# Feed-forward gates one place sooner and the Gelus moved ahead of the output copies of unit 1, in a two-network attention kernel

## The chip, the cores and the metric

The kernel runs on one core of a Trainium2 chip. The metric is device time in microseconds (us) of one execution. The runs shown are three, and their median is the time before.

## What is computed

The input x is 16 sequences of 128 tokens with 128 channels. Four blocks follow one another: a small cross-attention, a network of six layers, a second cross-attention, and a network of two layers. The change is in the feed-forward of the first network, whose layer is this (shortened):

```
for i in range(6):
    x = attn_layer(shift_tokens(x), Wqkv[i], q_scale[i], k_scale[i], Wo[i]) + x
    x = ffn_layer(shift_tokens(x), ln_g[i], ln_b[i], W1[i], b1[i], W2[i], b2[i]) + x

def attn_layer(x, ...):            # 16 heads of 64, windows of 32 tokens
    q, k, v = split(x @ Wqkv)      # l2norm, scale, rotary on q and k
    return local_attention(q, k, v) @ Wo

def ffn_layer(x, ...):             # DIM_INNER = 341
    xn = layernorm(x) * g + bln
    a, gate = split(xn @ W1 + b1)
    return a * gelu(gate) @ W2 + b2
```

All of it is float32.

## The kernel before

Every engine runs a program written out by hand, and the engines meet by semaphores alone. The first network runs as 96 pairs (6 layers of 16 sequences) in a software pipeline of steps. Step s starts pair s and works at the same time on pairs s-1, s-2 and s-3. A pair has two units, 0 and 1, of eight heads each. All five engines have a function `step_0(s)` that lists their work of a step in order.

TensorE (`step_0`, from L962) issues in step s: keys and queries of unit 0 for pair s (L710), values of unit 0 for s-2, the transposes of the probabilities of unit 1 for s-3 (L776), slot 0 of the feed-forward, the turn of q of unit 0 for s-1 (`turn`, L731), scores (L761, L767) and values (L790) of unit 1, keys and queries of unit 1 (L710), the output projection of s-3 (`project_out`, L823), slot 1 of the feed-forward, the turn of k of unit 0 (L731), probabilities of unit 0 (L776), values of unit 1 (L710), slot 2 of the feed-forward, the turns of k and q of unit 1 (L731, eight transposes), and scores and values of unit 0 (L767, L790).

ScalarE (`step_0`, from L1633) issues in step s: the exponents of unit 0 (`exponents_all`, L1578, eight activations, each with a read of its accumulator), a copy of the values (L1598), a copy of the turned probabilities (L1586), two squares (L1549), the copy of the turned q of unit 0 (`turned`, L1555), the output copies of unit 1 (`outputs(1, s-3)`, L1609, two halves), an activation for the feed-forward where the step has one (L1617, L1624), the exponents of unit 1, two squares, the copy of the turned k of unit 0, the copies L1586 and L1598, the two turned copies of unit 1, and last the output copies of unit 0.

Three of its waits matter here. TensorE begins `project_out` of s-3 only when `outputs(1, s-3)` is done (AT["oe"][1]). It begins the turn of k of unit 1 only when the turned k of unit 0 has left bank 6 (AT["kte"][0]). It begins the values of unit 0 of the next step only when `outputs(0, s-2)` is done (AT["oe"][0]), and the scores of unit 1 of the next step when the exponents of unit 0 have been read from banks 3 and 4.

The feed-forward of four sequences (a group, f = 0 to 23) takes four steps, by the counter c = (s-7) % 4, and shares PSUM bank 2 with a Newton iteration of VectorE:

- c = 0: mean (L835), down-projection of the group before (L877), variance (L841).
- c = 1: slot 0 the broadcast of the inverse deviation (L849); slot 2 gate 0 (`ff_gate`, L859, one product of 128x512 as two matmul records), which VectorE copies to SBUF (L2252).
- c = 2: slot 0 gate 1, slot 1 gate 2. At the end of the step, after the turned copies and before `outputs(0, s-2)`, ScalarE applies the three Gelus (`ff_gelu`, L1631). A Gelu needs another activation table than the exponents: a load ahead of the Gelus and one ahead of the next exponents.
- c = 3: the three up-projections (L868), one a slot, which VectorE multiplies by the Gelus (L2258).

22 groups (f = 0 to 21) run through all four steps while every pair is live; group 22 runs in the last steps, and group 23 in a list by hand (`between`) beside the second cross-attention. `normal_free` makes a product in bank 2 wait for the Newton iteration of the step before, and `ff_done` makes the Newton iteration wait until VectorE has copied the product before it.

```python
if c == 2 and f >= 0:
    ff_gelu(f)            # ScalarE, L1672: behind turned(1, s-1, 0)
if live(s - 2):
    outputs(0, s - 2)
```

Of the kernel before, what the change touches and what calls it, by code (L numbers as in the profile page):

```python
# [63 lines left out]
def build(nc, A, out):  # L64
# [9 lines left out]
    with ExitStack() as ctx:  # L74
# [234 lines left out]
        def g_broadcast(pe, n, k, o):  # L309

            pe.wait_ge(ln_rsqrt, (n + 3) * RSQ)
            pe_broadcast(k, o)
# [263 lines left out]
        def _(pe):  # L576
# [125 lines left out]
            def pe_phase(ph):  # L702
# [191 lines left out]
                def feed_forward_0(s, slot_):  # L894

                    if 1 <= s < 7:
                        group_norm(s, slot_)
                    c, f, before = ff_phase(ph, s)
                    if c == 0 and f >= 0 and slot_ == 0:
                        ff_mean(f, s)  # L900
                    if c == 0 and before >= 0 and slot_ == 1:
                        ff_down(before, s)
                    if c == 0 and f >= 0 and slot_ == 2:
                        ff_var(f)
                    if c == 1 and f >= 0 and slot_ == 0:
                        ff_broadcast(f, s)
                    if c == 1 and f >= 0 and slot_ == 2:
                        ff_gate(f, 0, s)
                    if c == 2 and f >= 0 and slot_ < 2:
                        ff_gate(f, 1 + slot_, s)  # L910
                    if c == 3 and f >= 0:
                        ff_up(f, slot_, s)

# [410 lines left out]
            def between(s, part):  # L1324

                if (s, part) == (1, 1):
                    ff0(99, 0)
                    ff0(99, 1)
                if (s, part) == (1, 2):
                    ff0(99, 2)  # L1330
                if (s, part) == (2, 1):
                    ff0(100, 0)
                    pe.wait_ge(FF["outer"], 3)
                    g_mean(pe, 6, 2, 6)
                if (s, part) == (2, 2):
                    g_var(pe, 6, 2, 6)
                    ff0(100, 2)
                if (s, part) == (3, 0):
                    g_broadcast(pe, 6, 2, 6)
                    ff0(101, 0)  # L1340
                if (s, part) == (3, 1):
                    ff0(101, 1)
                if s == 4:
                    ff0(102, part)
                if (s, part) == (5, 0):
                    ff0(103, 1)
                if (s, part) == (5, 1):
                    pe.wait_ge(FF["outer"], 4)
                    g_mean(pe, 7, 3, 2)
                if (s, part) == (5, 2):  # L1350
                    g_var(pe, 7, 3, 2)
                if (s, part) == (6, 1):
                    g_broadcast(pe, 7, 3, 2)
                if s in (7, 9):
                    n = 8 + (s - 7) // 2
                    if part == 0:
                        pe.wait_ge(LN["xn"], NBLK + n)
                        pe.wait_ge(YP["gt"], 8 * (n - 7))
                        g_mean(pe, n, n - 8, 2)
                    if part == 1:  # L1360
                        g_var(pe, n, n - 8, 2)
                    if part == 2:
                        g_broadcast(pe, n, n - 8, 2)
# [87 lines left out]
        def _(act):  # L1451
# [89 lines left out]
            def act_phase(ph):  # L1541
# [92 lines left out]
                def step_0(s):  # L1634
                    c, f, before = ff_phase(ph, s)
                    if live(s - 2):
                        exponents_all(0, s - 2)
                        values(0, s - 2)
                    if live(s - 3):
                        probs_all(1, s - 3)  # L1640
                    if live(s):
                        square(0, s, 1)
                        square(0, s, 0)
                    if s == 0:
                        gate_weights()
                    if live(s - 1):
                        turned(0, s - 1, 0)
                    if live(s - 3):
                        outputs(1, s - 3)
                    if s in (1, 3, 5):  # L1650
                        g_square(act, (s + 1) // 2, (s + 1) // 2)
                    if c == 0 and f >= 0:
                        ff_square(f)
                    if c == 1 and f >= 0:
                        ff_affine(f)
                    if live(s - 2):
                        exponents_all(1, s - 2)
                    if live(s):
                        square(1, s, 1)
                        square(1, s, 0)  # L1660
                    if live(s - 1):
                        turned(0, s - 1, 1)
                    if s == hi:
                        for k in range(2):
                            g_square(act, 4 + k, k)
                    if live(s - 2):
                        probs_all(0, s - 2)
                        values(1, s - 2)
                    if live(s - 1):
                        turned(1, s - 1, 1)  # L1670
                        turned(1, s - 1, 0)
                    if c == 2 and f >= 0:  # L1672
                        ff_gelu(f)
                    if live(s - 2):
                        outputs(0, s - 2)

# [357 lines left out]
        def _(dve):  # L2034
# [76 lines left out]
            def dve_phase(ph):  # L2111
# [27 lines left out]
                def ff_done(s):  # L2139

                    c, f, before = ff_phase(ph, s)
                    if f < 0 or c < 0:
                        at(dve, FF["z"], before + 1)
                    elif ni == 0 and c == 0:
                        dve.wait_ge(FF["rstd"], RSQ * (f + 1))
                    elif c == (3 if ni == 0 else 1):
                        dve.wait_ge(FF["hid"], 3 * f + 3)
                    else:
                        dve.wait_ge(FF["ge"], 3 * f + (3 if c == 2 else 1))

                n_s, n_b, n_c = (bank[2][:, 64 + 32 * k:96 + 32 * k].rearrange("p (i n) -> p i n", i=2) for k in range(3))

# [124 lines left out]
                def feed_forward_0(s, slot_):  # L2277

                    if 1 <= s < 7:
                        group_norm(s, slot_)  # L2280
                    c, f, before = ff_phase(ph, s)
                    if c == 0 and f >= 0 and slot_ == 0:
                        ff_centre(f)
                    if c == 0 and before >= 0 and slot_ == 1:
                        ff_close(before)
                    if c == 0 and f >= 0 and slot_ == 2:
                        ff_newton(f)
                    if c == 1 and f >= 0 and slot_ == 0:
                        ff_normalise(f)
                    if c == 1 and f >= 0 and slot_ == 2:  # L2290
                        ff_gate(f, 0)
                    if c == 2 and f >= 0 and slot_ < 2:
                        ff_gate(f, 1 + slot_)
                    if c == 3 and f >= 0:
                        ff_hidden(f, slot_)

# [300 lines left out]
            def between(s, part):  # L2597

                if (s, part) == (1, 1):
                    ff0(99, 0)  # L2600
                    ff0(99, 1)
                    outer(PHASES[0], 2)
                if (s, part) == (1, 2):
                    ff0(99, 2)
                if (s, part) == (2, 1):
                    ff0(100, 0)
                    g_centre(dve, 6, 2, 6)
                if (s, part) == (2, 2):
                    g_newton(dve, 6, 2, 6)
                    ff0(100, 2)  # L2610
                if (s, part) == (3, 0):
                    g_normalise(dve, 6, 2, 6)
                    ff0(101, 0)
                if (s, part) == (3, 1):
                    ff0(101, 1)
                if s == 4:
                    ff0(102, part)
                if (s, part) == (5, 0):
                    ff0(103, 1)
                    outer(PHASES[0], 3)  # L2620
                if (s, part) == (5, 1):
                    g_centre(dve, 7, 3, 2)
                if (s, part) == (5, 2):
                    g_newton(dve, 7, 3, 2)
                if (s, part) == (6, 1):
                    g_normalise(dve, 7, 3, 2)
                if s in (7, 9):
                    n = 8 + (s - 7) // 2
                    if part == 0:
                        g_centre(dve, n, n - 8, 2)  # L2630
                    if part == 1:
                        g_newton(dve, n, n - 8, 2)
                    if part == 2:
                        g_normalise(dve, n, n - 8, 2)
# [63 lines left out]
```

## Time and profile before

| | |
|---|---|
| time before, median of 3 runs | 2301.66 us (2299.51 to 2307.42) |
| the profiled execution | 2299.02 us |
| its span | 2297.2 us |
| TensorE busy | 2124.9 us, 93% |
| VectorE busy | 1760.9 us, 77% |
| ScalarE busy | 1712.2 us, 75% |
| GpSimd busy | 1340.2 us, 58% |
| granted TensorE clock, mean | 0.987 |

The span is the time from the first to the last instruction of the profiled execution; the 1.8 us between it and the execution's own time lie outside the instructions. Busy time of an engine is the sum over its instructions. Matmuls overlap the one before a little, so two rows of the timeline can start before the row above has ended. An idle time stands in brackets with what ended it.

### The profile page before, as it was taken

Reading aid. Unit: us, or ns where it says so; the run is one execution under the profiler, and the core shown is the slowest. Engines: PE = TensorE matmul, PEld = TensorE weight load, DVE = VectorE, ACT = ScalarE, POOL = GpSimd, SP = SyncE. Lnnn points to the kernel's source line nnn. Section 1 sums busy time; section 2 is a strip of 40 time slices with the busy share of each in tenths; the row PEclk is TensorE's granted clock in tenths of the full one; section 3 lists DMA queues with packets and bytes.
Section 4 is the critical chain, followed back from the end, with each engine's and each line's share of the span. In section 5 each row is a group of like instructions: output and inputs, shape, how many; then the busy total and the mean of one; then the engine's idle time right before and its main releaser. Section 6 shows DMA issues by size and latency. Waiting matters only on the chain. (4 is left out here: it accounts for less than half of the span.)

```text
span 2297.2 us, 88445 instructions
## 1 busy us (share of the span) xinstructions
PE 2124.9 (93%) x33790; PEld 1456.7 (63%) x33790; DVE 1760.9 (77%) x4953; ACT 1712.2 (75%) x5916; POOL 1340.2 (58%) x1270
## 2 busy tenths in 40 slices
PE   7988999999999999999999999999999886899997
PEld 5656666666666666666666666666666564666665
DVE  4988877778777878777778777877777478788873
ACT  3767788787787877787887777887788543778784
POOL 1337666666666666665676566666666124766660
PEclk8999999999999999999999999999999998999999
DMA  4001221112211222112211122111221100000001
GB/s 112 4 3 39 70 58 45 41 46 67 57 43 39 64 51 57 39 43 61 57 46 42 43 65 60 46 39 45 52 53 43 48 10 10 13 13 16 13 9 28
DMA packets 144799, 96.93 MB, mean 42 GB/s; under 512 B 61976, under 2 KB 137408, under 8 KB 144384
## 3 DMA queue, kind: packets, MB, share of 16 engines
q1 hardware_dynamic: 143232, 91.02, 15.5%
q8 instruction: 274, 4.49, 0.8%
q14 instruction: 141, 1.16, 0.2%
q10 hardware_dynamic: 1152, 0.26, 0.1%
HBM read 23.11 MB, written 1.05 MB: 11 GB/s over the span
## 5 line engine op out<-in xcount | busy, mean ns | idle before, releaser
L710 PE MATMUL bank<-wqkv,hs 128*128 128x512 f32 x1344 | 666.7, 614 | 19.3 <-ACT arena L1609 13.7
L1931 POOL TENSOR_TENSOR arena<-arena,rnorm 128x512 f32<-128x512 f32 x448 | 455.5, 1046 | 388.5 <-DVE rnorm L2180 387.3
L1924 POOL TENSOR_TENSOR arena<-arena 128x512 f32<-128x512 f32 x448 | 568.0, 1275 | 132.5 <-DVE arena L2129 132.2
L1578 ACT ACTIVATE arena<-bank,amx 128x64 f32<-128x64 f32 x1536 | 458.8, 336 | 8.5 <-DVE amx L2195 8.3
L2124 DVE TENSOR_TENSOR arena<-bank,rot 128x512 f32<-128x512 f32 x448 | 306.9, 685 | 82.7 <-PE bank L710 79.0
L1555 ACT ACTIVATE arena<-bank 128x512 f32<-128x512 f32 x448 | 264.4, 617 | 132.0 <-PE bank L731 130.9
L710 PEld LDWEIGHTS bank<-wqkv,hs 128*128 128x128 f32 x1344 | 228.6, 191 | 203.8 <-issue 154.9
L1578 ACT ACTIVATION_READ_ACCUMULATOR arena<-bank,amx 128x1 f32 x1536 | 352.3, 229 | 0.0
L2129 DVE TENSOR_TENSOR arena<-bank,rot 128x256 f32<-128x256 f32 x896 | 334.0, 414 | 0.0
L731 PEld LDWEIGHTS bank<-ident,arena 128*128 128x128 f32 x1792 | 212.6, 142 | 152.8 <-issue 128.3
L2136 DVE TENSOR_REDUCE ss<-arena 128x8 f32<-128x512 f32 x448 | 283.4, 670 | 32.5 <-ACT arena L1549 32.3
L1549 ACT ACTIVATE arena<-bank 128x512 f32<-128x512 f32 x448 | 265.9, 647 | 42.0 <-DVE arena L2129 41.2
L1938 POOL TENSOR_TENSOR arena<-arena,ainv 128x512 f32<-128x512 f32 x192 | 200.7, 1045 | 164.9 <-DVE ainv L2203 164.7
L731 PE MATMUL bank<-ident,arena 128*128 128x128 f32 x1792 | 251.5, 274 | 14.1 <-POOL arena L1931 6.4
L1609 ACT ACTIVATE arena<-bank 128x256 f32<-128x256 f32 x384 | 127.2, 387 | 174.6 <-PE bank L790 173.7
L823 PEld LDWEIGHTS bank<-arena,wo 128*128 128x128 f32 x1792 | 221.6, 194 | 55.1 <-issue 48.1
L790 PE MATMUL bank<-arena 64*64 64x32 f32 (+1 forms) x9216 | 186.1, 221 | 49.0 <-issue 47.6
L823 PE MATMUL bank<-arena,wo 128*128 128x128 f32 x1792 | 226.9, 279 | 3.0 <-ACT arena L1609 2.6
L790 PEld LDWEIGHTS bank<-arena 64*64 64x64 f32 x9216 | 160.6, 134 | 71.0 <-issue 54.5
L2195 DVE TENSOR_REDUCE amx<-bank 128x4 f32<-128x256 f32 x384 | 143.8, 416 | 39.8 <-PE bank L767 39.2
L767 PE MATMUL bank<-arena 64*32 64x64 f32 (+1 forms) x12288 | 168.8, 217 | 0.0
L767 PEld LDWEIGHTS bank<-arena 64*32 64x32 f32 x12288 | 154.9, 105 | 0.3
(213 smaller groups left out, 3229.8 us busy)
## 6 DMA issues: line engine op xcount, KB each, us to landing
arena<-arena SPq DMA_DIRECT2D x768, 64.0 KB
wqkv<-in_L_ffn_Wqkv_dram SPq DMA_DIRECT2D x24, 256.0 KB
hs<-z SPq DMA_DIRECT2D x128, 32.0 KB, 1.8
hs<-z SPq DMA_DIRECT2D x128, 31.8 KB, 1.9
fx<-z SPq DMA_DIRECT2D x31, 128.0 KB, 2.2
fx<-z SPq DMA_DIRECT2D x31, 127.0 KB, 2.5
wqkv<-in_L_ffn_Wqkv_dram SPq DMA_DIRECT2D x24, 128.0 KB
w<-in_L_ffn_W_dram SPq DMA_DIRECT2D x6, 341.0 KB
```

Source lines behind the costliest of these rows:

```text
L710: nc.tensor.matmul(bank[o][:], src[:], wqkv[w][:, off:off + 512], start=True, stop=True).then_inc(AT[name] if part < 2 else AT[name][i], 1)
L731: mm = nc.tensor.transpose(bank4[o][:, j, :], rc[i][c][p % 2][:, j * P:(j + 1) * P], ident[:])
L767: mm = nc.tensor.matmul(bank[3 + g][q:q + 32, DH * j:DH * j + n], q_t[i][rows, P * j + q:P * j + q + 32], k_t[i][rows, P * j + key:P * j + ...
L790: mm = nc.tensor.matmul(bank4[7 - half][to:to + DH, j, q0:q1], src[g][rows, DH * h:DH * h + DH], pbt[i][0][rows, h * P + q0:h * P + q1], s ...
L823: mm = nc.tensor.matmul(bank4[7][:, 0, :], wo[w][:, i, j, :] if ni == 0 else wo[w][:, j // 2, j % 2, :], o_t[i][:, j * P:(j + 1) * P], sta ...
L1549: nc.scalar.activation(sq[i][c], bank[c][:], ACT.Square).then_inc(AT["sqk" if c else "sqq"], 1)
L1578: ins = nc.scalar.activation(pb[i][0][p % 2][:, h * DH:(h + 1) * DH], bank[3 + g][:, j * DH:(j + 1) * DH], ACT.Exp, bias=amx[p % 2][:, i, ...
L1924: nc.gpsimd.tensor_tensor(t, t, rs[i][c], ALU.add).then_inc(AT["ak" if c else "aq"][i], 1)
L1931: nc.gpsimd.tensor_tensor(t, t, rnorm[p % 2][:, i, HU * c:HU * c + HU].unsqueeze(2).to_broadcast([P, HU, DH]), ALU.mult).then_inc(AT["mk" ...
L2124: nc.vector.tensor_tensor(heads(rc[i][c][p % 2]), src, r[:, 2 * c, :].unsqueeze(1).to_broadcast([P, HU, DH]), ALU.mult)
L2129: ins = nc.vector.tensor_tensor(dst, src[:, :, (1 - a) * hd:(2 - a) * hd], r[:, 2 * c + 1, a * hd:(a + 1) * hd].unsqueeze(1).to_broadcast( ...
L2136: nc.vector.tensor_reduce(ss[:, i, HU * c:HU * c + HU], heads(sq[i][c]), AX.X, ALU.add).then_inc(AT["ssk" if c else "ssq"], 1)
```

## The change

The gates move by one slot: gate 0 and gate 1 run in step c = 1, slots 1 and 2, and gate 2 in step c = 2, slot 0. The same is done on TensorE and VectorE. On ScalarE the three Gelus move, within the step c = 2, from behind the turned copies of unit 1 to the place between `turned(0, s-1, 0)` and `outputs(1, s-3)`. The waits of the Newton iteration for the copies of the gates follow. In the list by hand of group 23 gates 1 and 2 move by one place and its Gelus stay. No operation is added or left out.

```diff
@@ TensorE feed_forward_0, and the same with ff_gate(f, c) on VectorE
-                    if c == 1 and f >= 0 and slot_ == 2:
-                        ff_gate(f, 0, s)
-                    if c == 2 and f >= 0 and slot_ < 2:
-                        ff_gate(f, 1 + slot_, s)
+                    if c == 1 and f >= 0 and slot_ > 0:
+                        ff_gate(f, slot_ - 1, s)
+                    if c == 2 and f >= 0 and slot_ == 0:
+                        ff_gate(f, 2, s)
@@ TensorE between, and the same on VectorE
                     g_var(pe, 6, 2, 6)
-                    ff0(100, 2)
+                    ff0(100, 1)
                 if (s, part) == (3, 0):
                     g_broadcast(pe, 6, 2, 6)
+                    ff0(100, 2)
+                if (s, part) == (3, 1):
                     ff0(101, 0)
-                if (s, part) == (3, 1):
-                    ff0(101, 1)
@@ ScalarE step_0
                         turned(0, s - 1, 0)
+                    if c == 2 and f >= 0:
+                        ff_gelu(f)
                     if live(s - 3):
                         outputs(1, s - 3)
...
                         turned(1, s - 1, 1)
                         turned(1, s - 1, 0)
-                    if c == 2 and f >= 0:
-                        ff_gelu(f)
                     if live(s - 2):
                         outputs(0, s - 2)
@@ VectorE ff_done
+                    elif ni == 0 and c == 2:
+                        dve.wait_ge(FF["ge"], 3 * f + 3)
                     else:
-                        dve.wait_ge(FF["ge"], 3 * f + (3 if c == 2 else 1))
+                        dve.wait_ge(FF["ge"], 3 * f + (2 if ni == 0 else 1))
```

## Rows read from the trace of the kernel before

**Rows 1.** Who waited for whom, TensorE, 280 to 1800 us: total, times, longest.

```profile
PE bank L790 <- issue: 42.6, 62, 1.8
PE bank L761 <- issue: 19.4, 22, 1.0
PE bank L710 <- ACT arena L1609: 13.7, 16, 0.9
```

**Rows 2.** Timeline of TensorE, step 45 (c = 2) and next: start, us, what, [idle].

```profile
905.61 0.60 PE L731 MATMUL bank<-ident,arena 128*128 128x128 f32 x4
...
909.76 1.95 PE L823 MATMUL bank<-arena,wo 128*128 128x128 f32 x16
911.54 1.02 PE L859 MATMUL bank<-arena,w 128*85 128x512 f32 x2
...
914.14 1.04 PE L731 MATMUL bank<-ident,arena 128*128 128x128 f32 x8
...
919.76 1.13 PE L710 MATMUL bank<-wqkv,hs 128*128 128x512 f32 x2 [0.86 <-ACT arena L1609]
...
922.02 0.60 PE L731 MATMUL bank<-ident,arena 128*128 128x128 f32 x4
923.60 0.30 PE L761 MATMUL bank<-mask_b,ident_b 64*32 64x256 bf16 x8 [0.98 <-issue]
...
924.73 0.90 PE L790 MATMUL bank<-arena 64*64 64x64 f32 x48 [0.17 <-issue]
```

**Rows 3.** Timeline of ScalarE over the same stretch.

```profile
905.58 1.16 ACT L1549 ACTIVATE arena<-bank 128x512 f32<-128x512 f32 x2
906.53 0.70 ACT L1555 ACTIVATE arena<-bank 128x512 f32<-128x512 f32 x1
908.08 0.66 ACT L1609 ACTIVATE arena<-bank 128x256 f32<-128x256 f32 x2 [0.84 <-PE bank L790]
...
913.04 0.60 ACT L1555 ACTIVATE arena<-bank 128x512 f32<-128x512 f32 x1 [0.69 <-PE bank L731]
...
915.93 1.28 ACT L1631 ACT_TABLE_LOAD   x1
917.23 1.95 ACT L1631 ACTIVATE arena<-arena,b 128x512 f32<-128x512 f32 x3
919.08 0.63 ACT L1609 ACTIVATE arena<-bank 128x256 f32<-128x256 f32 x2
919.73 1.28 ACT L1578 ACT_TABLE_LOAD   x1
921.02 0.31 ACT L1578 ACTIVATE arena<-bank,amx 128x64 f32<-128x64 f32 x1
...
923.35 0.63 ACT L1598 ACTIVATE arena<-bank 128x512 f32<-128x512 f32 x1
```

**Rows 4.** Timeline of VectorE and of GpSimd over the same stretch, one row each.

```profile
905.92 0.64 DVE L2252 COPY arena<-bank 128x512 f32<-128x512 f32 x1
...
918.81 4.05 POOL L1931 TENSOR_TENSOR arena<-arena,rnorm 128x512 f32<-128x512 f32 x4 [3.05 <-DVE rnorm L2180]
```

**Rows 5.** Timeline of TensorE in other steps: idle inside a run of L790.

```profile
303.00 0.67 PE L790 MATMUL bank<-arena 64*64 64x32 f32 x32 [1.16 <-issue]
...
499.95 0.42 PE L790 MATMUL bank<-arena 64*64 64x32 f32 x11 [0.71 <-issue]
...
1063.13 0.86 PE L790 MATMUL bank<-arena 64*64 64x64 f32 x24 [1.82 <-issue]
...
1746.40 0.66 PE L790 MATMUL bank<-arena 64*64 64x32 f32 x28 [1.39 <-issue]
...
1751.98 0.30 PE L761 MATMUL bank<-mask_b,ident_b 64*32 64x256 bf16 x8 [0.42 <-issue]
```

**Rows 6.** Windows of two steps c = 3: length, busy by engine, granted clock.

```profile
848.14:868.13 19.99, 16.65 (x305) 10.93 (x299) 13.71 (x38) 15.86 (x53) 11.06 (x10) 1.00 0.24 61
1054.49:1076.54 22.05, 19.45 (x301) 12.92 (x299) 12.77 (x31) 14.44 (x51) 11.05 (x10) 0.85 0.24 66
```

More of the change, by code:

```diff
@@ L2289, in feed_forward_0 @@
                         ff_normalise(f)
[L2290 to L2293, printed above, removed]
+                    if c == 1 and f >= 0 and slot_ > 0:
+                        ff_gate(f, slot_ - 1)
+                    if c == 2 and f >= 0 and slot_ == 0:
+                        ff_gate(f, 2)
                     if c == 3 and f >= 0:
@@ L2609, in between @@
                     g_newton(dve, 6, 2, 6)
-                    ff0(100, 2)
+                    ff0(100, 1)
                 if (s, part) == (3, 0):
                     g_normalise(dve, 6, 2, 6)
+                    ff0(100, 2)
+                if (s, part) == (3, 1):
                     ff0(101, 0)
-                if (s, part) == (3, 1):
-                    ff0(101, 1)
                 if s == 4:
```

## The prediction

> **What bounds the kernel now.** I read the waits of TensorE first, since it is the busiest engine and the chain that ended last runs mostly over it. Over the steady part of the first network it waits for little. [rows 1] hold nearly all of it: idle inside and before L790, 62 times, which I take to be late code (below); 22 waits before the scores (L761), one for each of the 22 full groups; and 16 waits of L710 for the output copies. The last two kinds sit at one place, just behind the Gelus. So the pace is TensorE's own work, and the Gelus are one of the few things that break it.
>
> Then I read the two timelines of one pass, step 45 (c = 2) and the step after it. On TensorE [rows 2] the reader is to see an unbroken run from the turn of q of unit 0 at 905.61 to the keys of the next step, and then three idles: 0.86 us before the values product at 919.76, 0.98 before the scores at 923.60, 0.17 before the values at 924.73. On ScalarE [rows 3] the copy of the turned q ends at 906.53 + 0.70 = 907.23; it waits 0.84 us for the output copies, later 0.69 us for the turned k of unit 0; from the table load at 915.93 on it has no idle, and TensorE waits for it.
>
> What the Gelus cost today: idle 0.86 + 0.98 + 0.17 = 2.01 us. An idle also costs the overlap that unbroken matmuls have (909.76 + 1.95 = 911.71, yet L859 starts at 911.54: 0.17; 0.07 before L761 and L790), so some 0.3 more: **2.31 us a pass**. That is the most that the change can give back.
>
> **The change, part by part.** All is worked on the pass of [rows 2, 3]; I looked at the 22 passes, and copy and turns keep their distances in 19 of them, within 0.1 us.
>
> Gates. A gate costs TensorE 1.02 - 0.16 = 0.86 us [rows 2]. One gate leaves step c = 2 (slot 1) and one more is in step c = 1. TensorE paces both places, so work is neither saved nor added; all of the pass from slot 1 of c = 1 to slot 1 of c = 2 is 0.86 us later, and what follows is 0.86 earlier against it. VectorE's copies move along. The copy in slot 0 of c = 2 is done at 905.92 + 0.64 = 906.56 [rows 4], before 907.23, so the Gelus find their third input ready at the new place: no wait for it. In slot 1 of c = 1 the gate needs the affine activation, which ScalarE does ahead of the exponents while TensorE still has its output projection to run: nothing, and if that cover went, at most one copy's length. SyncE's transfers of the unit-1 values wait for a copy that will be some 2 us later, and its queue has no transfer behind them that is needed before that; GpSimd starts its four products at 918.81 [rows 4], follows VectorE's Newton iteration, and would start about 2 us later, still before TensorE turns its result a step on. Both nothing, as long as this stays near 2 us.
>
> The Gelus at the new place. Times as if slot 0 of c = 2 had not moved:
> - load and Gelus: the next copy starts 919.08 - 915.93 = 3.15 us after the load starts [rows 3]. The load starts at 907.25, so the output copies start at 910.40 and end at 911.03 (0.63).
> - TensorE's projection starts 0.05 us behind such a copy (919.08 + 0.63 = 919.71, then 919.76): 911.08 in place of 909.76. **First new wait, 1.32 us.** ScalarE's idle of 0.84 us was all that the place offered, against 3.15.
> - the table load for the exponents, 1.29 us, now stands ahead of those of unit 1: they start at 912.34, take 923.35 - 921.02 = 2.33, then two squares, 906.53 - 905.58 = 0.95, then the turned k of unit 0, 0.70: done at 916.32.
> - TensorE needs that copy gone from bank 6 before the turns at 914.14. Without the gate it would be there at 914.14 - 0.86 = 913.28; it goes on at 916.37. **Both waits together are 3.09 us**, the second 1.77.
>
> From there no wait is left. The turn and what follows come 2.23 us later than now. The outputs of unit 0 are copied as soon as TensorE has them, without Gelus or load ahead, and so are the exponents of the next step. From the turns at 914.14 to the values at 924.73 are 10.59 us, of which 2.31 are the waits of today: 8.28. So the values start at 916.37 + 8.28 = 924.65 against 924.73.
>
> **Sum of a pass**: waits of 3.09 in place of 2.31, so +0.78 us. 22 passes: **+17 us**.
>
> Late code. Idle inside a run of L790 shows no releaser but "issue", and comes at places of the program where TensorE issues its densest instructions; I take it that the instructions are late. Two places matter. In 3 passes such an idle (0.71 at 499.95, [rows 5]; the other two are alike) stands before the first new wait, which then is shorter by as much: -2 us in all. In 7 passes (the first 1.16, the last 1.39, [rows 5]) it stands in the last values run of step c = 2. Today it is free: the wait for ScalarE behind it shrinks, as at 1751.98, where 0.42 is left of 0.98. In the new order ScalarE has nothing late behind it, so it counts in full, 7 x 1.2 = +8 us. The bounds: absorbed, 0, if the wait at the turns 2 us ahead lets the code catch up; in full, +8. I take the full price, since the nearest row, 1063.13, shows 1.82 us of it in a step c = 3 just behind the waits that 923.60 and 924.73 stand for, so waits ahead did not shorten it.
>
> Groups 22 and 23 run where few pairs are live, and the Gelus of 23 stay; I bound them by one pass's waits either way, -2 to +3 us, and take 0.
>
> Sum: 17 - 2 + 8 = **+23 us** on the profiled execution's 2299.02, 2322 us. The median of the runs is 2.6 us above that execution; I put half of it on: **2323 us**.
>
> Table loads. The rows show the load itself, 1.28 us, and 0.02 us on either side of it [rows 3]. The Trainium skill, "ScalarE: Activation LUTs", section "What ACT_TABLE_LOAD costs", adds a drain of some 1.38 us to each switch. By that rule the two switches in the new chain would make each pass 2.76 us longer, an estimate from that page of some +61 us more. The trace has the load's length as the page has it, and not the drain.
>
> **The rivals.**
> - *The waits go away, faster.* The change gives back the 2.31 us of each pass and the new place costs TensorE nothing: -2.31 x 22 = -51 us, 2250; with the first of the two waits left, 1.32 x 22 = +29 us stands against it: -22 us, 2278. It decides at bank 6: the turned k of unit 0 must be copied by 913.28. For it speaks that ScalarE idles 0.84 + 0.69 us just here [rows 3], and more in three passes. Against it: 4.4 us of Gelus and load go in, and exponents, squares and copy behind them have fixed lengths. It wants the chain 3 us shorter than its rows. Chance 0.09.
> - *A wash.* Waits as worked out, but the new idles let the late code catch up, in the 7 passes and at some others of the 62 places (42.6 us in all, [rows 1]): 17 - 2 - 10 = +5 us, 2305. Against it is 1063.13 [rows 5]. Chance 0.10.
> - *The clock.* TensorE now stands still once for over 1.3 and once for 1.8 us within 6 us. The granted clock has fallen to half (1.2 from 2.4 GHz) in a step c = 3 that began with idles: 22.05 us at a mean of 0.85 against 19.99 at full clock, 2.06 us [rows 6]. If every third pass gets such a stretch, +15 us more: 2338. The Trainium skill, "TensorE: Matmul & The Clock Gate", section "What's actually happening", has the gate closed by default and opened by activity, which speaks against the change; the trace shows it rarely at idles of this size. Chance 0.10.
> - *The chain as worked out*: +13 to +28 us. Chance 0.70. The last 0.01 is for the drain.
>
> **How the numbers follow.** A measurement of this kernel can tell 0.3%, some 7 us, from no change. Slower by more: 0.70 + 0.10 + a small part of the wash, 0.81. Within: 0.09. Faster: 0.10. The range leaves out the fast rival and the end of the clock's: low is the wash with the late code mostly absorbed, 2304; high is 2323 with the outer bound of groups 22 and 23 and some four clock stretches (8 us), 2334.
>
> **What would show each step.** In the changed trace: the waits before L761 (22 of 0.98) and of L710 for L1609 gone; 22 new waits of L823 for L1609 of 1.0 to 1.3 us, and 22 of L731 for L1555 of 1.5 to 1.8; idle of ScalarE before L1609 smaller, and new idle of it before the output copies of unit 0, some 1 us a pass; the table loads still 1.28 us each. Step c = 1 some 0.9 us longer, c = 2 some 2.2 longer, c = 3 some 2.3 shorter. The forecast is wrong if the turns of unit 1 don't wait in c = 2, if L790's idle shrinks by over 8 us in all, or if steps c = 0 and 3 change by more than these waits.

## The result and the profile after

The change makes the kernel slower: 2319.9 us (median of 4 runs, 2318.8 to 2325.4) against 2303.2 us for the kernel before in the same comparison, a ratio of 1.0076 with a 95% interval of 1.0057 to 1.0095. That is +17.5 us on 2302. The profiled execution of the changed kernel, 2325.4 us with a span of 2322.4, is the slowest of its four, so a part of what its trace shows over [rows 1 to 6] is that run's own.

The waits of TensorE in the changed kernel, from 280 to 1820 us (in total, times, longest), answer to [rows 1]:

```profile
PE bank L790 <- issue: 35.9, 40, 1.8
PE bank L731 <- ACT arena L1555: 30.7, 22, 1.4
PE bank L823 <- ACT arena L1609: 25.6, 22, 1.5
PE bank L731 <- POOL arena L1931: 4.3, 14, 0.6
...
PE bank L710 <- ACT arena L1609: 0.8, 1, 0.8
```

The 22 waits before L761 are gone, and of the 16 of L710 for the output copies one is left. In their place stand two kinds that were not there, 22 of each: the output projection (L823) waits for the output copies of unit 1, and the turn of k of unit 1 (L731) waits for ScalarE's copy (L1555) of the turned k of unit 0.

The timeline of TensorE in the changed kernel, step 45 (c = 2) and into step 46, answers to [rows 2]: start, us, what, and idle in brackets.

```profile
919.23 0.60 PE L731 MATMUL bank<-ident,arena 128*128 128x128 f32 x4
...
921.56 1.98 PE L710 MATMUL bank<-wqkv,hs 128*128 128x512 f32 x4
924.78 2.02 PE L823 MATMUL bank<-arena,wo 128*128 128x128 f32 x16 [1.24 <-ACT arena L1609]
...
927.52 1.02 PE L710 MATMUL bank<-wqkv,hs 128*128 128x512 f32 x2
929.95 1.14 PE L731 MATMUL bank<-ident,arena 128*128 128x128 f32 x8 [1.41 <-ACT arena L1555]
...
932.86 2.84 PE L710 MATMUL bank<-wqkv,hs 128*128 128x512 f32 x6
...
937.36 0.30 PE L761 MATMUL bank<-mask_b,ident_b 64*32 64x256 bf16 x8
...
938.34 0.90 PE L790 MATMUL bank<-arena 64*64 64x64 f32 x48
```

The reader is to see that the idle has moved, not gone: before it was 0.86, 0.98 and 0.17 us at the start of step 46, now it is 1.24 and 1.41 in step 45, and step 46 runs without a break. ScalarE over the same stretch, which answers to [rows 3]:

```profile
920.15 0.70 ACT L1555 ACTIVATE arena<-bank 128x512 f32<-128x512 f32 x1
920.86 1.28 ACT L1631 ACT_TABLE_LOAD   x1
922.15 1.95 ACT L1631 ACTIVATE arena<-arena,b 128x512 f32<-128x512 f32 x3
924.01 0.63 ACT L1609 ACTIVATE arena<-bank 128x256 f32<-128x256 f32 x2
924.66 1.28 ACT L1578 ACT_TABLE_LOAD   x1
925.95 0.31 ACT L1578 ACTIVATE arena<-bank,amx 128x64 f32<-128x64 f32 x1
...
928.28 1.12 ACT L1549 ACTIVATE arena<-bank 128x512 f32<-128x512 f32 x2
929.24 0.66 ACT L1555 ACTIVATE arena<-bank 128x512 f32<-128x512 f32 x1
...
932.99 0.66 ACT L1609 ACTIVATE arena<-bank 128x256 f32<-128x256 f32 x2 [1.15 <-PE bank L790]
```

From 920.15 to the copy that ends at 929.24 + 0.66 = 929.90 ScalarE has no idle; TensorE goes on at 929.95. Where the Gelus stood it now idles 1.15 us. Steps 44, 45 and 46 of the changed kernel as windows (length, busy by engine, granted clock):

```profile
898.80:915.26 16.46, 16.17 (x306) 11.00 (x301) 14.34 (x42) 13.11 (x49) 12.43 (x16) 1.00 0.20 52
915.26:932.86 17.60, 14.95 (x299) 10.09 (x295) 12.17 (x35) 16.41 (x53) 11.01 (x10) 1.00 0.13 31
932.86:949.49 16.63, 16.29 (x304) 11.00 (x298) 14.07 (x41) 12.35 (x48) 11.03 (x10) 1.00 0.24 56
```

Over the 22 passes the mean length of a step, by c = 0, 1, 2, 3, was 18.09, 15.96, 15.84 and 18.65 us before and is 18.15, 16.90, 18.11 and 16.45 now: +0.06, +0.94, +2.27, -2.20, in sum +1.07 us a pass, or 24 us over the 22 passes of these two profiled executions.

### The profile page after: what moved, and what is told of

The parts are those of the page before. It is cut to its first block and busy times, and to the rows that moved or that the text cites. A ratio compares the mean times of both kernels' runs of the same rounds, so it can differ in the third digit from the quotient of the medians.

```text
span 2322.4 us, 88445 instructions
## 1 busy us (share of the span) xinstructions
PE 2132.2 (92%) x33790; PEld 1454.1 (63%) x33790; DVE 1764.1 (76%) x4953; ACT 1711.3 (74%) x5916; POOL 1340.8 (58%) x1270
## 5 line engine op out<-in xcount | busy, mean ns | idle before, releaser
L1931 POOL TENSOR_TENSOR arena<-arena,rnorm 128x512 f32<-128x512 f32 x448 | 455.7, 1046 | 403.5 <-DVE rnorm L2182 402.3
L710 PE MATMUL bank<-wqkv,hs 128*128 128x512 f32 x1344 | 666.6, 616 | 6.6 <-ACT arena L1549 2.5
L1555 ACT ACTIVATE arena<-bank 128x512 f32<-128x512 f32 x448 | 266.5, 626 | 131.3 <-PE bank L731 130.2
L710 PEld LDWEIGHTS bank<-wqkv,hs 128*128 128x128 f32 x1344 | 231.1, 192 | 187.2 <-issue 166.0
L731 PEld LDWEIGHTS bank<-ident,arena 128*128 128x128 f32 x1792 | 210.7, 142 | 191.3 <-issue 121.5
L731 PE MATMUL bank<-ident,arena 128*128 128x128 f32 x1792 | 254.3, 276 | 44.3 <-ACT arena L1555 33.7
L823 PEld LDWEIGHTS bank<-arena,wo 128*128 128x128 f32 x1792 | 220.1, 195 | 89.0 <-ACT arena L1609 46.5
L823 PE MATMUL bank<-arena,wo 128*128 128x128 f32 x1792 | 228.8, 280 | 29.1 <-ACT arena L1609 28.6
L790 PE MATMUL bank<-arena 64*64 64x32 f32 (+1 forms) x9216 | 187.1, 221 | 43.0 <-issue 40.6
L790 PEld LDWEIGHTS bank<-arena 64*64 64x64 f32 x9216 | 160.7, 134 | 64.6 <-issue 46.1
```

The costliest lines, as they stand in the source:

```text
L710: nc.tensor.matmul(bank[o][:], src[:], wqkv[w][:, off:off + 512], start=True, stop=True).then_inc(AT[name] if part < 2 else AT[name][i], 1)
L731: mm = nc.tensor.transpose(bank4[o][:, j, :], rc[i][c][p % 2][:, j * P:(j + 1) * P], ident[:])
L790: mm = nc.tensor.matmul(bank4[7 - half][to:to + DH, j, q0:q1], src[g][rows, DH * h:DH * h + DH], pbt[i][0][rows, h * P + q0:h * P + q1], s ...
L823: mm = nc.tensor.matmul(bank4[7][:, 0, :], wo[w][:, i, j, :] if ni == 0 else wo[w][:, j // 2, j % 2, :], o_t[i][:, j * P:(j + 1) * P], sta ...
L1555: nc.scalar.activation((k_t if c else q_t)[i], bank[5 + c][:], ACT.Copy).then_inc(AT["kte" if c else "qte"][i], 1)
L1931: nc.gpsimd.tensor_tensor(t, t, rnorm[p % 2][:, i, HU * c:HU * c + HU].unsqueeze(2).to_broadcast([P, HU, DH]), ALU.mult).then_inc(AT["mk" ...
```

## The experiments

My theory: the length of ScalarE's queue between two copies that TensorE waits for decides, and the new place makes two waits of 3.0 us a pass out of 2.3. The main rivals: the gates are at fault, or the late output projection alone, or TensorE's late code and clock. The times of the experiments are ratios to the kernel before in the same comparison, times 2302 us where a difference in us is given.

### Gates alone

```diff
 (the changed kernel)
                         turned(0, s - 1, 0)
-                    if c == 2 and f >= 0:
-                        ff_gelu(f)
...
                         turned(1, s - 1, 0)
+                    if c == 2 and f >= 0:
+                        ff_gelu(f)
```

> Gates one place sooner, Gelus left at their old place. Theory (the Gelus in ScalarE's queue cause the waits; a gate is work that TensorE does at either place): the three idles behind the Gelus stay at 0.86, 0.98 and 0.17 us, step c = 1 is 0.86 us longer and step c = 2 as much shorter, and the time is that of the kernel before, 2303 us, within 4. Rival (the gates are at fault: with gate 2 gone from slot 1 of c = 2 TensorE has nothing to do there and runs into waits): a good part of the change's +17 us shows already, 2311 or more.

Measured: 2302.0 us, ratio 1.0015 (1.0000 to 1.0029), at its middle value a fifth of the loss, and not told from none. Its waits of TensorE, 280 to 1800 us:

```profile
PE bank L790 <- issue: 42.3, 63, 2.0
PE bank L761 <- issue: 18.9, 22, 1.0
PE bank L710 <- ACT arena L1609: 13.8, 16, 0.9
```

They are those of [rows 1] within 0.5 us. Step c = 1 is 0.87 us longer in the mean, c = 2 0.81 shorter. The gates make none of the new waits, and at most 7 of the 17.5 us; a part of these can be the clock, for this trace has 5 stretches at half clock, 20.5 us, where the kernel before has 2 of 10.2.

### The Gelus one place later

```diff
 (the changed kernel)
                         turned(0, s - 1, 0)
-                    if c == 2 and f >= 0:
-                        ff_gelu(f)
                     if live(s - 3):
                         outputs(1, s - 3)
+                    if c == 2 and f >= 0:
+                        ff_gelu(f)
```

> As the changed kernel, but the Gelus stand one place later on ScalarE, behind the output copies of unit 1 and ahead of its exponents. Theory (the length of ScalarE's queue up to the turned k of unit 0 decides, not the first wait): the wait of L823 for L1609 is gone, but ScalarE idles its 0.84 us ahead of the copies again and the turn waits longer, 1.41 + 1.40 + 0.85 = some 3.6 us a pass in place of two waits of 1.24 and 1.41, so 0.7 to 0.9 us a pass more: 2320 + 17 = 2337 us. Rival (what costs is that the output copies come late, and the projection with them): without that wait the pass is 1.2 us shorter, 2320 - 27 = 2293 us.

Measured: 2378.1 us, ratio 1.0357 (1.0329 to 1.0384). The rival is out: with no wait of the projection for the output copies left, the kernel is 65 us slower than the changed one by the two ratios. But my own number, 17 us more than the changed kernel, is 48 us short. Its timeline of TensorE in step 45:

```profile
939.39 0.60 PE L731 MATMUL bank<-ident,arena 128*128 128x128 f32 x4
...
946.17 1.02 PE L710 MATMUL bank<-wqkv,hs 128*128 128x512 f32 x2
951.04 1.61 PE L731 MATMUL bank<-ident,arena 128*128 128x128 f32 x8 [3.85 <-ACT arena L1555]
...
953.86 1.34 PE L790 MATMUL bank<-arena 64*64 64x64 f32 x48
955.13 2.84 PE L710 MATMUL bank<-wqkv,hs 128*128 128x512 f32 x6
```

and a window over the same step, begun 0.6 us late (length, busy by engine, granted clock):

```profile
936.00:955.70 19.70, 15.85 (x296) 11.11 (x295) 12.55 (x37) 16.57 (x54) 11.03 (x10) 0.91 0.13 30
```

The wait is 3.85 us in one piece, where I had summed some 3.6. From the turn of q of unit 0 to the turns of unit 1 it is 951.04 - 939.39 = 11.65 us, against 929.95 - 919.23 = 10.72 in the changed kernel: 0.93 us more, near the 0.7 to 0.9 expected, so the wait itself was priced about right and the miss lies behind it. There the eight transposes take 1.61 us, where they take 1.14 in the changed kernel, and the values run 1.34 where it takes 0.90, and the granted clock of the step is 0.91: TensorE has fallen to 1.2 GHz for a part of it. The mean granted clock is 0.84 to 0.94 in all 22 steps c = 2 of this kernel, and 1.00 in all 22 of the changed one. Between 287 and 1760 us its trace has 22 stretches at half clock, 119.5 us together; the kernel before has 2 and the changed one 3, in sum 10.2 us in either. So what I had as a rival for the change came true here, in every pass.

### The table loads away, at the new and at the old place

```diff
 (the changed kernel; and the same in the kernel before)
-  nc.scalar.activation(gl[c][0:w, :], gl[c][0:w, :], ACT.Gelu, ...
+  nc.scalar.activation(gl[c][0:w, :], gl[c][0:w, :], ACT.Gelu if ni else ACT.Identity, ...
```

> As the changed kernel, with Identity in place of the three Gelus of the first network, so that both table loads of a pass are gone (the Gelu of the first network is left out of the computation). Theory: ScalarE's chain is 2 x 1.29 us shorter, the wait of L823 vanishes and that before the turn falls to 0.4 or less, so 22 x 2.6 = 57 us come off: 2263 us, and up to 8 less if the late code in the last values run is then hidden. Rival (the waits come from the three activations' place and not from what they take, or from the clock): less than 20 us come off.

> As the kernel before, with Identity in place of the three Gelus of the first network (the Gelu of the first network is left out of the computation). Theory: the loads are 2.57 us of ScalarE's chain and the waits today 2.31, so these vanish wholly: 2303 - 51 = 2252 us; the idle inside L790 at the end of step c = 2 in 7 passes, which the waits hid, then counts for some 8 us: 2260 us. Rival (late code is hidden anyway): 2252 us or less.

Measured: at the new place 2258.5 us, ratio 0.9826 (0.9807 to 0.9846), which is 0.025 or 57.5 us under the changed kernel, as forecast; at the old place 2244.5 us, ratio 0.9771 (0.9743 to 0.9799), 53 us under the kernel before. The waits of TensorE, 280 to 1800 us, first at the new place:

```profile
PE bank L790 <- issue: 38.4, 44, 2.0
PE bank L731 <- POOL arena L1931: 4.9, 15, 0.9
PE bank L823 <- ACT arena L1609: 2.6, 3, 0.9
```

then at the old place:

```profile
PE bank L790 <- issue: 31.6, 42, 2.1
PE bank L731 <- POOL arena L1931: 4.6, 14, 0.8
PE bank L823 <- ACT arena L1609: 2.6, 3, 0.9
```

With the same three activations in the queue and 2.57 us of loads taken out, every wait of L731 for ScalarE and all but 3 of L823 are gone, and so are those before L761. The 3 of L823 that are left stand in the last steps of the network, and the kernel before has them too (at 1791, 1810 and 1822 us). So the loads make the waits at either place, and the rival of the first run (less than 20 us) is out. It also bounds what any place for the Gelus could bring: some 53 us.

At the old place the forecast was a miss. It was 2260 us, 43 under the kernel before; 53 came (46 to 59), which is the rival's number, 2252 or less. The rival's reason does not fit: at the 7 places the late code still shows as 6.8 us of idle, so it was not hidden. But at 5 places early in steps c = 3 it fell from 7.6 to 3.4 us, and 51 - 6.8 + 4.2 = 48 us lies within the interval.

One thing this pair leaves open. No wait that the Gelus make is left in either kernel, and yet the new order is 12.7 us slower than the old (ratios 0.9826 and 0.9771), with an uncertainty of some 8 us. In the two traces the late code at L790 is 6.8 us more (38.4 against 31.6), and between 287 and 1760 us there are 6 stretches at half clock, 20.5 us, against 1 of 6.8; whether the new order causes either was not tested. So the loads account for all the waits, but these two times alone, 57.5 against 53 us, do not show where the 17.5 us of loss come from: that rests on the rows of the waits and on the lengths of the steps.

### ScalarE's copies ahead of its squares

```diff
 (the changed kernel, steps c == 2)
+                    if late:
+                        turned(0, s - 1, 1)
+                        probs_all(0, s - 2)
                     if live(s):
                         square(1, s, 1)
                         square(1, s, 0)
```

> As the changed kernel, but in steps c = 2 ScalarE copies the turned k of unit 0 and the turned probabilities of unit 0 ahead of its two squares of unit 1 instead of behind them. Theory (the second wait is for bank 6 to be emptied, and its length is that of ScalarE's queue up to this copy): the wait of L731 for L1555 shrinks by the two squares, 0.95 us, to some 0.45 us, the wait of L823 for L1609 stays at 1.24; 22 x 0.95 = 21 us come off, 2299 us. Rival (ScalarE as a whole is the bound of these steps, and work moved in its queue only moves the wait): the wait shows up behind the squares, and the time stays at 2320 us within 5.

Measured: 2316.0 us, ratio 1.0060 (1.0038 to 1.0082), not told apart from the changed kernel. Its waits of TensorE:

```profile
PE bank L790 <- issue: 34.3, 42, 2.0
PE bank L823 <- ACT arena L1609: 25.1, 22, 1.5
PE bank L790 <- ACT arena L1555: 9.8, 22, 0.5
PE bank L731 <- ACT arena L1555: 9.1, 21, 0.4
```

The wait before the turn fell from 1.41 to 0.43 us, as the theory says, so it is bank 6 that TensorE waits for there. But 0.45 us came back at once as a new wait, of the last values product for the turned k of unit 1, which I had not foreseen. That leaves 0.53 us a pass, 12 us. The mean steps of the two traces agree (0.52 us a pass), while the ratios show 4 us with an uncertainty of some 7 on each side. Both theories had a part of it; the 21 us were a miss.

### Filling the waits of the kernel before

If the waits of the kernel before are ScalarE's queue, they can be filled. Three kernels, each with the edits of the one before it:

```diff
 (the kernel before; TensorE, steps c == 3)
                         turn(0, s - 1, 0, "mq", "qt")
+                    if c == 3 and f >= 0:
+                        ff_up(f, 1, s)
...
-                    feed_forward_0(s, 1)
+                    if not (c == 3 and f >= 0):
+                        feed_forward_0(s, 1)
...
 (VectorE, steps c == 3: ff_hidden(f, 0) ahead of row_sum_all(0, s - 2))
```

> As the kernel before, but in steps c = 3 the second up-projection stands ahead of the scores of unit 1, in TensorE's wait for the exponents, instead of in slot 1, and VectorE multiplies the first up-projection ahead of its row sums. Theory (today's waits are ScalarE's queue behind the Gelus, and TensorE can fill them): the 0.98 us ahead of L761 becomes 0.4 us ahead of that product, 0.86 us of work goes out of the rest of the step, 0.78 us a pass: 17 us come off, 2285 us. Rival (TensorE's stream is late by its code, not by ScalarE): nothing comes off, 2302 us within 4.

Measured: 2290.8 us, ratio 0.9964 (0.9951 to 0.9976), 8 us less (6 to 11). Faster, but half of what was expected.

```diff
 (VectorE, steps c == 2, behind newton(s, 0, 3); ScalarE leaves it out)
+                        dve.wait_ge(AT["qt"][1], s)
+                        at(dve, AT["s"], un(1, s - 2))
+                        nc.vector.tensor_copy(q_t[1], bank[5][:]).then_inc(AT["qte"][1], 1)
```

> As the run before it, and in steps c = 2 VectorE, in its idle of 0.86 us before the row maxima, copies the turned q of unit 1 in ScalarE's place. Theory: ScalarE's queue ahead of the Gelus and the exponents is 0.5 us shorter, and so is the wait, 22 x 0.5 = 11 us more come off: 2274 us. Rival (VectorE's copy delays its Newton iteration and the products of GpSimd behind it): the time is that of the run before or above it, with a new wait of L731 for L1931.

Measured: 2283.3 us, ratio 0.9931 (0.9912 to 0.9950), 16 us less than before in all; this step gave 7.6 of the 11, with an uncertainty of some 5.

```diff
 (TensorE; third is c == 3 and f >= 0, and slot 0 is then left out)
                         queries(0, s)
+                    if third:
+                        ff_up(f, 0, s)
...
 (VectorE, steps c == 3: ff_hidden(f, 0) ahead of rotate(0, s, 1))
```

> As the kernel with the second up-projection in the wait and the copy on VectorE, and in steps c = 3 the first up-projection stands right behind the queries of unit 0, in TensorE's wait for the output copies (0.37 us there), and VectorE multiplies it ahead of its rotations. Theory (what is left, 0.37 and 0.50 us a pass, is waiting that work can fill, until the exponents of unit 0 on ScalarE are the bound, some 0.5 us sooner than now): 22 x 0.5 = 11 us come off 2283, 2272 us, and the wait of L868 for VectorE is gone. Rival (the rotations, which then come some 1.8 us later, are on the path to ScalarE's squares and exponents): the time stays at 2283 us or goes up by up to 15, with a new wait of TensorE in steps c = 3 behind unit 1's keys.

Measured: 2276.5 us, ratio 0.9884 (0.9846 to 0.9922), 27 us less than before (18 to 36). This step gave some 11 us, as expected, but with an uncertainty of some 10. The kernel beats both the one before and the changed one. The waits of TensorE in the first and in the last of the three:

```profile
PE bank L790 <- issue: 41.9, 44, 2.3
PE bank L710 <- ACT arena L1613: 13.7, 16, 0.9
PE bank L868 <- DVE arena L2262: 11.0, 22, 0.5
```

```profile
PE bank L790 <- issue: 44.3, 59, 1.9
PE bank L761 <- issue: 9.8, 15, 0.7
PE bank L731 <- POOL arena L1940: 4.8, 16, 0.8
```

In the first the 22 waits before L761 have become 22 of 0.5 us before the moved product, which waits there for VectorE. In the last that one and those of L710 are gone, and what is left stands before L761 again, for the exponents (in step 46 the last of them is read by 923.68, and L761 starts at 923.78): ScalarE's queue is the bound, as the expectation had it. Why the first gave 8 and not 17 us is only partly told: the idle inside and before L790, 42.6 us in [rows 1] with 22 small waits of 0.17 in it, is 41.9 here without them, so late code took some 3 us back; and that profiled execution, 2299.7 us and the slowest of its ten, had 5 stretches at half clock, 17.1 us, against 2.

## Why the prediction was right, point by point

**What bounds the kernel.** That TensorE's own work sets the pace and the Gelus break it held: without the table loads the old order is 53 us faster, and the waits of 2.31 us in 22 passes were worth 51. Nothing was forecast for SyncE and GpSimd, and nothing came: TensorE waited 14 times for GpSimd's L1931, 4.3 us in all, against 14 times and 4.8 us before.

**The gates.** Forecast: step c = 1 longer and the rest sooner by 0.86 us, nothing in sum. Gates alone gave 0.87 and 0.81 in the means, and 1.0015 as the ratio. Right; up to 0.3% is not excluded.

**The two new waits.** Forecast 1.32 and 1.77 us, 3.09 together. Measured by the same reckoning: the projection starts at 924.78 where it could at 921.56 + 1.98 - 0.16 = 923.38, so 1.40; the turn at 929.95 where it could at 927.52 + 0.86 = 928.38, so 1.57. Together 2.97, and the two runs behind them are 0.07 and 0.10 us longer than in [rows 2], so 3.14. Each of the two is off by up to 0.2 us, their sum is not. The prediction's own sign for the second, idles of 1.5 to 1.8 us, missed: they are 1.41. The chain of ScalarE was right: from the turn of q to the turns of unit 1 it is 929.95 - 919.23 = 10.72 us, forecast 916.37 - 905.61 = 10.76.

**The sum of a pass.** From the turn of q of unit 0 to the values of unit 1 in the next step it was 924.73 - 905.61 = 19.12 us [rows 2] and is 938.34 - 919.23 = 19.11; with the gate's 0.86 us moved ahead of it that is +0.85, forecast +0.78.

**Table loads.** Both loads are 1.28 us at the new place, with 0.01 to 0.02 us on either side: the drain that the Trainium skill, "ScalarE: Activation LUTs", section "What ACT_TABLE_LOAD costs", adds is not there, and 61 us more did not come. The trace agrees with the page on the load's length alone.

**Late code.** Forecast: -2 us at 3 places, +8 at 7. I summed the idle inside runs of L790 in the steps 9 to 93 of both traces. In the 3 places ahead of the first wait it was 1.9 us and is now hidden. In the 7 places at the end of step c = 2 it is now 10.1 us, in full, where it was 8.1 and, as the prediction has it, hidden. These are rows of the changed kernel's timeline of TensorE, the first of such a place, the second of another kind:

```profile
583.90 0.31 PE L790 MATMUL bank<-arena 64*64 64x32 f32 x8 [1.81 <-issue]
...
1078.72 0.55 PE L790 MATMUL bank<-arena 64*64 64x64 f32 x24 [1.09 <-issue]
```

The second is the place of 1063.13 in [rows 5], early in a step c = 3: 1.82 us before, 1.09 now. There are 5 of these, in sum 7.6 us before and 3.5 now. This I had not foreseen: -4 us.

**The total.** With 22 x 0.85 = 19 us for the passes, 19 - 2 + 10 - 4 = +23 us by these rows, forecast +23. The steps of the two profiled executions say +24 for the 22 passes, the medians +17.5 with some 4 either way; the profiled execution of the changed kernel is 5.5 us above its median. The forecast of 2323 us is 3 us over the 2320 measured. Two terms were mis-sized, and they offset each other, which is luck: a pass by +0.07 us, 2 us in all, and the late code, +6 as forecast and +4 by its rows. The +8 for it at the 7 places was an assumption that no run tested by itself, and where a run did depend on it (the old place without table loads) the time was 10 us under the forecast.

**The rivals.** The fast one asked for the turned k of unit 0 to be copied 3 us sooner than its rows allow; the rows held. The clock: the changed kernel has 3 stretches at half clock in the steady part against 2, of 10.2 us in sum each, so it took no part. The wash asked for late code that the new idles would hide at the 7 places; it was in full.

## What to carry to other kernels

An idle time of an engine is room for no more than its own length: 0.84 us of idle does not take 3.15 us of table load and Gelus and another load of 1.28 behind them. Before a piece of work is moved into a gap, follow the queue behind it to every copy that a busier engine waits for, and write down by when each must be done; here the second such copy, not the first, cost more, and in one experiment a third came up. Where the waits come from a queue that can't be shortened, fill them with the busy engine's own later work: that, with one copy given to an idle engine, was worth 27 us here (18 to 36).

## What the runs showed of the hardware

**One long wait is another thing than two short ones.** Two idles of TensorE of 1.24 and 1.41 us with 4 us of work between them left the granted clock at 1.00 in the step c = 2 of all 22 passes; one idle of 3.85 us brought it down in each of the 22, and the work behind it ran at half clock (eight transposes in 1.61 us instead of 1.14). Between these two traces a mean pass differs by 2.25 us, and 0.93 of that is the longer way to the turns in step 45. From the turns to the keys of the next step it is 955.13 - 951.04 = 4.09 us against 932.86 - 929.95 = 2.91, and the 1.18 us of difference stand where the clock is at half. That the length of the idle brings the clock down, and not its place, was not tested by itself.

**The idle inside L790 goes with the loading of instructions.** In the kernel before, 40 idles of over 0.3 us stand before a matmul of L790 between 280 and 1800 us, and all 40 end 2.2 to 2.9 us after a 16 KB transfer of the instruction queue has begun; in the changed kernel it is all 37 of 37. Such stretches behind these transfers make up about an eighth of the time, so chance would give 5. This supports what the prediction took for granted, that the instructions are late.

**A short wait just ahead does not hide it.** At the 7 places at the end of step c = 2 the idle is 10.1 us in the changed kernel, with a wait of 1.41 us ahead, and 8.1, 8.7, 6.8 and 11.1 us in four kernels with no wait there (the one before, gates alone, and those without table loads at the old and the new place). With a wait of 3.85 us ahead it is all but gone, 0.6 us. At the 5 places early in step c = 3 the picture is mixed: 7.6 us in the kernel before and with the gates alone, which have TensorE waiting just ahead; 3.5, 3.2 and 3.4 us in the changed kernel and in the two without table loads, which have no wait there; but 5.7 us in the kernel with ScalarE's copies first, which has none either. I read this as code that is fetched by the place where the engine's queue stands; no run tested that by itself, and it stays open.
